# Attention values of a whole unit in one visit of TensorE instead of two half visits

## What is computed

```python
x = x + attn_a(layernorm(x))      # 32 heads of 16, rotary, latent K and V, all keys seen
x = x + ffn(layernorm(x))         # one 512x512 matrix plus eight low-rank terms
x = x + attn_b(layernorm(x))      # 32 heads of 16, causal, a bias that grows with distance
x = x + ffn(layernorm(x))

scores = einsum('bqhd,bkhd->bhqk', q, k) * scale
probs = softmax(scores)
attn = einsum('bhqk,bkhd->bqhd', probs, v)
```

## Time and profile before

| | us |
|---|---|
| median of 3 runs | 1733.36 |
| lowest and highest of them | 1726.22, 1735.23 |
| the profiled execution, device time | 1734.83 |
| its span in the trace | 1732.9 |
| attention a in the trace, first exponential to last | 202.6 to 865.9 |
| attention b in the trace, first exponential to last | 1156.5 to 1625.6 |

### The profile page before, as it was taken

How to read it: one execution, slowest core, us unless ns; L and a number is a source line. 1 busy time by engine, 2 the same in 40 slices (tenths; PEclk the granted TensorE clock), 3 DMA queues, 4 the chain that set the end, 5 groups by cost and what they waited for, 6 DMA issues and landing times. The chain is left out here.

```text
span 1732.9 us, 32976 instructions
## 1 busy us (share of the span) xinstructions
PE 1634.3 (94%) x13040; PEld 838.2 (48%) x13040; DVE 1390.5 (80%) x2959; ACT 968.0 (56%) x1095; POOL 213.3 (12%) x272
## 2 busy tenths in 40 slices
PE   6898999999999999999999999999999999999899
PEld 4554333333333333333344767654545454545587
DVE  3776799999999999999548364469898989888486
ACT  3433287888888888887821111126666666665420
POOL 3332200000000000000023021010031210000233
PEclk9999699999999999999999999989999999998999
DMA  7665434334333333332140433665463646372231
GB/s 220 224 183 190 91 58 81 58 64 63 61 64 62 62 62 69 57 60 60 58 160 25 146 93 106 217 159 102 75 98 66 107 67 105 62 106 68 67 121 73
DMA packets 116801, 167.58 MB, mean 97 GB/s; under 512 B 20772, under 2 KB 58036, under 8 KB 116532
## 3 DMA queue, kind: packets, MB, share of 16 engines
q1 hardware_dynamic: 115176, 160.99, 40.9%
q0 software_dynamic: 1472, 4.49, 1.3%
HBM read 100.41 MB, written 64.50 MB: 95 GB/s over the span
## 5 line engine op out<-in xcount | busy, mean ns | idle before, releaser
L358 DVE TENSOR_REDUCE mxp<-ps_m 128x1 f32<-128x512 f32 x1280 | 802.1, 685 | 54.0 <-PE ps_m L324 49.3
L703 ACT ACTIVATE a_p<-a_ps_s 128x1024 f32<-128x1024 f32 x512 | 524.8, 1026 | 154.9 <-PE a_ps_s L616 140.2
L703 ACT ACTIVATE b_p<-b_ps_s 128x1024 f32<-128x1024 f32 (+1 forms) x320 | 295.1, 939 | 161.5 <-PE b_ps_s L616 158.3
L355 DVE CUSTOM_DVE_ANT_0 ps_m<-ps_m,b_masks 128x128 f32<-128x128 f32 (+3 forms) x512 | 240.3, 516 | 46.9 <-PE ps_m L324 42.3
L324 PE MATMUL ps_m<-slot_qk 62*128 62x512 f32 (+3 forms) x624 | 229.8, 451 | 11.9 <-DVE mxp L358 9.0
L324 PE MATMUL ps_m<-a_slot_qk 62*128 62x512 f32 x640 | 235.2, 448 | 0.9 <-DVE mxp L358 0.9
L616 PE MATMUL a_ps_s<-a_slot_qk 64*128 64x512 f32 x640 | 234.4, 444 | 0.0
L640 PE MATMUL a_ps_o<-a_p,a_slot_v 128*32 128x256 f32 x2560 | 207.6, 391 | 8.8 <-ACT second_v L694 8.6
L616 PEld LDWEIGHTS a_ps_s<-a_slot_qk 64*128 64x128 f32 x640 | 95.5, 185 | 131.8 <-issue 131.4
L281 POOL CAST cparts<-negm 128x16 fp32r<-128x16 f32 x64 | 12.7, 198 | 1099.2 <-DVE negm L364 1099.2
L616 PE MATMUL a_ps_s<-slot_qk 64*128 64x512 f32 x384 | 137.7, 456 | 0.0
(11 more groups left out here) (217 smaller groups left out, 2341.9 us busy)
## 6 DMA issues: line engine op xcount, KB each, us to landing
va_tokens<-w_o SPq DMA_DIRECT2D x16, 512.0 KB, 2.7
ka_parts<-pa_parts SPq DMA_DIRECT2D x16, 512.0 KB, 3.0
qa_parts<-pa_parts SPq DMA_DIRECT2D x32, 256.0 KB, 3.7
kb_parts<-slot_memory SPq DMA_DIRECT2D x16, 512.0 KB, 4.1
qb_parts<-slot_memory SPq DMA_DIRECT2D x32, 256.0 KB, 3.4
vb_tokens<-w_proj SPq DMA_DIRECT2D x16, 512.0 KB, 2.9
a_slot_qk<-qa_parts SPq DMA_DIRECT2D x60, 128.0 KB, 4.1
a_slot_qk<-ka_parts SPq DMA_DIRECT2D x48, 128.0 KB, 6.8
```

The lines of the kernel that those rows point to most:

```text
L355: dve.tensor_tensor_reduce(from_, from_, mask_of_query[:, CHUNK - keys:], 1.0, LOWEST, ALU.add, ALU.max, accum_out=to).then_inc(piece_take ...
L358: dve.tensor_reduce(to, from_, AX.X, ALU.max).then_inc(piece_taken, 1)
L703: act.activation(p_sb[:, (2 * u + pair) % NP, :, off:CHUNK], ps_s[:, 2 * pair:2 * pair + 2, off:CHUNK], ACT.Exp, scale=scale).then_inc(exp ...
```

## The change

`values` loses its parameter `part`. One call does all blocks of a unit over all their columns, so a wide unit has four matmuls of 512 columns (8 in the trace) where it had twice four of 256. The call stands behind the second `half_unit` of the next unit. Nothing stands between the two `half_unit`s any more. Scores, pieces, exponentials, reductions, loads and stores keep their number, their sizes and their order on their engines. Narrow units of b had one visit before and have one now, in the same place.

```diff
-                def values(s, j, u, part):
+                def values(s, j, u):
                     qh, blocks = units[u]
-                    (kt, off, n, at) = blocks[0]
-                    if n == CHUNK:
-                        ranges = [(kt, off + part * CHUNK // 2, CHUNK // 2, at + part * CHUNK // 2)]
-                    else:
-                        ranges = blocks if part else []
                     pe.wait_ge(exp_done, s * NT + (2 * u + 2))
...
-                    for kt, off, n, at in ranges:
+                    for kt, off, n, at in blocks:
...
-                    if part:
-                        mm.then_inc(pv_done, 1)
+                    mm.then_inc(pv_done, 1)
...
                         half_unit(s, j, u, 0, lo, cut)
-                        values_behind(s, u, 0)
                         half_unit(s, j, u, 1, cut, hi)
-                        values_behind(s, u, 1)
+                        values_behind(s, u)
```

More of the change, by code:

```diff
@@ L618, in scores @@
                         mm.then_inc(score_ready, 1)
-                def values(s, j, u, part):
+                def values(s, j, u):
                     qh, blocks = units[u]
-                    (kt, off, n, at) = blocks[0]
-                    if n == CHUNK:
-                        ranges = [(kt, off + part * CHUNK // 2, CHUNK // 2, at + part * CHUNK // 2)]
-                    else:
-                        ranges = blocks if part else []
                     pe.wait_ge(exp_done, s * NT + (2 * u + 2))
-                    if u == 0 and part == 0:
+                    if u == 0:
                         wait_past(pe, v_loaded[j], loads(s) * 16)
-                    if u == first_of[qh] and part == 0:
+                    if u == first_of[qh]:
                         wait_past(pe, out_copied, 2 * s + qh)
-                    for kt, off, n, at in ranges:
-                        last = part == 1 and u == last_of[qh] and (kt, off, n, at) == ranges[-1]
+                    for kt, off, n, at in blocks:
+                        last = u == last_of[qh] and (kt, off, n, at) == blocks[-1]
                         for h in range(GH):
@@ L642, in values, with values_behind @@
                                            p_sb[:, (2 * u + h // 2) % NP, h % 2, at:at + n],
-                                           start=(u == first_of[qh] and part == 0), stop=last)
-                    if part:
-                        mm.then_inc(pv_done, 1)
-                def values_behind(s, u, part):
+                                           start=(u == first_of[qh]), stop=last)
+                    mm.then_inc(pv_done, 1)
+                def values_behind(s, u):
                     if u:
-                        values(s, s % SLOTS, u - 1, part)
+                        values(s, s % SLOTS, u - 1)
                     elif s and not causal:
-                        values(s - 1, (s - 1) % SLOTS, NU - 1, part)
+                        values(s - 1, (s - 1) % SLOTS, NU - 1)
                 def half_unit(s, j, u, pair, lo, hi):
@@ L668, in step @@
                         half_unit(s, j, u, 0, lo, cut)
-                        values_behind(s, u, 0)
                         half_unit(s, j, u, 1, cut, hi)
-                        values_behind(s, u, 1)
+                        values_behind(s, u)
                     if causal or s == NG - 1:
-                        values(s, j, NU - 1, 0)
-                        values(s, j, NU - 1, 1)
+                        values(s, j, NU - 1)
                 def keep_clock(columns):
```

## The result

| | before | changed |
|---|---|---|
| median, us | 1732.1 (6 runs) | 1777.9 (6 runs) |
| lowest and highest, us | 1726.2, 1735.2 | 1777.3, 1781.2 |
| ratio to before | | 1.0275, 95% interval 1.0249 to 1.0302 |
| span of the profiled execution, us | 1732.9 | 1775.8 |

The change costs 45.8 us. The forecast was 1779, slower, with a range of 1760 to 1798.

What follows compares the result with a forecast made beforehand. TensorE was taken to set the pace at 2.48 us a unit of a, VectorE close behind at 2.44. Terms of +34 (a) and +11 (b) on 1734.8 gave 1780, stated as 1779 against the median; range 1760 to 1798.

Steps and rivals of the forecast that it cites:

- The visit: Value matmuls of a wide unit on TensorE: 512 columns take 1.00 us, replacing two of 0.57 for 256 columns.
- Rival B: Wide unit of a: 512 columns cost only 0.78 us, the unit stays 2.48, time 1734 (1725 to 1742); chance 0.04.
- The chain: Plain unit of a: fourth piece waits for the first one's reduction and bank; steps sum to 2.70 us, from 2.48.
- The unit with a transposition: In a, the transposition also takes a bank and waits for the second piece: 3.09 us; eight units 21.99 against 20.88.
- The pairs without a visit between them: Four pairs in a unit of a start at 0, 0.34, 0.57, 0.80; TensorE alone gains 0.35 us a unit.
- rival A: Bursts don't bind and the saved change of form comes through: 1677, or 1700 to 1720 in part; chance 0.06.
- Attention b: Wide visits: unit 6 +0.31, unit 5 +0.45, other four 0; about +0.75 us a group, 15 groups, +11.
- The buffers of `p_sb`: Four buffers hide the longer distance from a unit's scores to its values; costed at nothing, up to 1.02 if failing.
- VectorE's idle time: Before reductions in a, waiting on pieces: rises from 5.4 us in 200 to about 18.
- The clock: Granted clock in 240 to 800 us: expected to stay at 1.00; below that would point to rival C.
- rival C: New waits in every unit make the clock fall, 5 us each time; two to eight more give 1790 to 1820; chance 0.06.
- The sum: Whole kernel: +34 for a and +11 for b, +45 on 1734.8 gives 1780; stated as 1779.

Runs made afterwards that it cites:

- short form of before: The kernel before with the pieces of attention a cut from 512 keys to 256: measured 1675.9 us.

## Why the prediction was right, point by point

- **The visit.** 512 columns were extrapolated to 1.00 from 256 and 384 (the rows give 0.79 for 384, the text 0.78, and 0.78 + 0.21 is 0.99; nothing hangs on it). Measured 0.99 to 1.00. The run with two narrow visits in a row shows the same 1.00. Rival B is out.
- **The chain.** Its steps in the changed kernel: first piece to reduction 0.54 (0.50 + 0.04 expected), reduction and restart 501.35 - 500.61 = 0.74 (0.69 + 0.05), to the values 0.43 (0.42), the visit 0.99. The unit is 2.70, as forecast. Three more runs follow the same sum: with the reduction at 0.43 and the step to the values at 0.31 the unit is 2.33, with 0.28 and 0.25 it is 2.14 (where ScalarE's loop is as long), and with a bank less, which changes nothing else, it is 3.31.
- **The unit with a transposition** was put at 3.09 and takes 3.14; eight units were put at 21.99 and take 22.15. So a was forecast at +34 and costs 36. Two small errors offset each other there: the first 15 groups cost 37.2 and not 33, and the last group, taken at about +1, is 1.2 shorter.
- **The pairs without a visit between them.** 500.07, 500.41, 500.65: steps of 0.34 and 0.24, as read in b. So the starts are as close as the gain of 0.35 needs, and the wait of 0.57 covers it, as the prediction put it; as time, the 0.35 was never seen whole. Of rival A's condition (a load done ahead) nothing is seen: the fourth load follows a reduction in all 173 units.
- **Attention b.** Units 5 and 6: +0.37 and +0.30, forecast +0.45 and +0.31. The sixth piece's wait was priced with a full reduction of 0.69 where the third piece has 384 columns and takes 0.61 with the read of its accumulator (1329.98 to 1330.59), so 0.08 too high. A group takes 30.1 us for 29.3, +0.8 where I had +0.75: the other four visits, put at 0 for want of a better number, add 0.15. The whole of b costs 8 and not 11: the last group, which has few pieces left, gains 1.4 us (19.2 for 20.6), and the groups at b's start and end run at half clock a little shorter (10.2 us each for 13.7). To count 15 groups and nothing beyond them was too simple.
- **The buffers of `p_sb`** were said to hide the longer distance from scores to values, at no cost. None of the waits of a's exponentials between 240 and 800 us ends with values.
- **VectorE's idle time** in 200 us of a was put at about 18 and is 16.5.
- **The clock** stayed at 1.00 in a and in the middle of b, so rival C had no part here. In the two-bank runs it fell in b.
- **The sum** is closer than its terms. That 1779 meets 1777.9 within about 1 us is partly luck: the errors just named have both signs. What is confirmed is the unit of 2.70 and the two units of b.

The expectations missed more often: 0.39 for the end of a short piece was wrong, the short form of before came out faster than its range, and both two-bank kernels slower than theirs, for the clock and b's waits were not in the sum. The prediction itself didn't lean on the 0.39, since its pieces are as long as the scores beside them. And of the 2.14 expected with the shortest pieces, the chain was right and "TensorE's own" was not.

## What to carry to other kernels

Here two engines that hand buffers to each other stayed in step while the work between hand-overs was spread evenly. Drawing the producer's other work together saved it a switch and made the hand-overs a burst, and the burst, longer than the number of buffers, put the consumer's latency into the producer's loop. Write down that loop, from the first hand-over of a burst to the restart of the last, before you trust the saved switch. The new order helped where the consumer's step was short, and at the one place where the engine waited for something else anyway; there it can be taken alone.

## What the runs showed of the hardware that I had not expected

- A 256-column piece, started together with a 512-column score in the other half of the rows, ended at 495.42 in its row, but its reduction started at 495.58, 0.04 behind the end of the score in front of it. The same kernel with 128 columns: VectorE starts 501.81 - 501.27 = 0.54 behind the start, though the piece's row is 0.32 long. In both, shortening the product brought its reader no earlier start while a longer one stood in front of it.
- Sixteen value matmuls of 256 columns in a row and eight of 512 both hold the array for 1.00 us. Here the split itself costs nothing that the rows show. The Trainium skill, "Perfetto Trace Analysis", section Matmuls, prefers larger matmuls; at these sizes no run here shows a gain by size. The prediction read the 1.00 for twice 0.57 as agreeing with it; since the two narrow visits in a row take the same 1.00, what saves is that the work stands together.
- Waits of TensorE of about half a microsecond in every unit left the clock at 1.00 in a, and so did the longer ones of the two-bank form (units of 3.31, 400 to 600 us). In b of that form the mean granted clock of a 200 us stretch was 0.72, though TensorE's rows cover 188.9 us of it, more than the 178.9 in a.
